# A transformer block on one core: the last batch's softmax denominators through TensorE, and new order lists

## Chip, core, metric

The kernel runs on one core of a Trainium2 chip. The metric is the device time of one execution in microseconds; lower is better. "Batch" is one of 32 sequences of 512 tokens with 256 features.

## The reference

```python
x = x + layernorm(attention(layernorm(x)))         # x: (32, 512, 256) float32
x = x + layernorm(ffn(layernorm(x)))

# attention, 16 heads of 16 features, weights 256x256 but W_down 256x64, W_up_k and W_up_v 64x256
q = x @ Wq
latent = (x @ Wk + x @ Wv) @ W_down_kv
k, v = latent @ W_up_k, latent @ W_up_v
scores = clip(q k^T / 16) * exp(-0.01 * 0.01 * |i - j|)      # 512 x 512 for each head
out = (softmax(scores) v) @ Wo

# ffn: Hadamard rotation, activations rounded to 4 bits per token, ternary weights
xh = x @ H
scale = max|xh| over the token / 7
out = (clip(round(xh / scale), -8, 7) * scale) @ ternary(weight).T
```

## The kernel before

Each engine walks its own list and meets the others at semaphores. A batch's attention is 32 **steps** (h = 0 to 31), four to a pair of heads: `scores` (L707) writes one unit of score blocks to PSUM; the unit of every fourth step holds the diagonal blocks, which VectorE multiplies by the decay (`weigh_diagonal`, L1253) and ScalarE turns into exponentials for two pairs together (`diag_exp`, L916); of the other units ScalarE takes the exponential straight from PSUM (`off_exp`, L909). Two halves of `scores_ps` alternate, so step h waits until the unit of step h - 2 has been read. `pv` (L720) multiplies four heads' exponentials (a quad) with v, in four pieces, one for each tile of 128 keys; the value matrix has an extra column of ones for each head, so row 16 of each head's 32 rows is the sum of its exponentials. VectorE copies a quad to `heads` (L1150).

Between the steps stand the other stages, of several batches at once: "pre" for the next batch (transposes `xT` L587, `lat` L595, `q` L603, `k` L614, `v` L625, with VectorE's weighting L1161, its cast L1168 and the split into two float16 parts on GpSimd L1038), "own" (scores, `pv`), "a" for the batch before (the last quad's `pv_end` and copy, the division by the sums, `y` L635 with Wo, layer norm, residual), "b" for the one before that (`x1T` L650, `x1_low` L1204, Hadamard `xh` L660, `act_scales`, rounding on ScalarE, `qintT` L669), and "c" (ternary product `z` L678, layer norm, residual, store). The tables TENSOR_STEPS, SCALAR_STEPS and VECTOR_STEPS say behind which step each engine does which piece; POOL_STEPS and SYNC_STEPS are plain sequences for one batch. Twenty-six batches run in a hardware loop of two, six are written out. Behind the last batch's scores the CLOSING lists take over: each entry is (stage, batches back from 32, half, part, piece), and the last batch (back = 1) goes in halves of two token tiles. Three PSUM banks serve the side stages in the loop, seven in the closing; `claim` waits until a bank's former holder has been taken. These banks follow from the order of the list; for the stages of the loop they are the same before and after.

**The division.** Softmax is divided by its sums after the product with v. The sums lie on one partition per head with 512 tokens along it. SyncE writes them to memory (`gather_den`, L462), loads them packed over 128 partitions (`pack_den`, L467), VectorE inverts them (`den_invert`, L1172), SyncE writes them back (`return_den`, L481) and loads them spread over the 16 rows of each head (`spread_den`, L489), and GpSimd multiplies (`heads_normalize`, L1043) the compacted heads (`compact`, L474). Then `heads_ready` lets `y` start. This is done for every batch, the last included.

## Time and profile before

| | |
|---|---|
| median of 3 runs | 1435.21 us (1431.94 to 1436.89) |
| the profiled execution | 1435.05 us, its span 1433.2 us |
| TensorE matmul busy | 1349.5 us, 94% of the span |
| TensorE weight load busy | 600.5 us, 42% |
| VectorE busy | 1179.9 us, 82% |
| ScalarE busy | 1098.2 us, 77% |
| GpSimd busy | 834.7 us, 58% |

The profile is of one execution. Times in its rows are microseconds from the start of the span. PE is TensorE's matmul, PEld its weight load, DVE VectorE, ACT ScalarE, POOL GpSimd, SPq SyncE's DMA queue, L a line of the kernel. A row of a timeline merges neighbouring instructions of one line: its length is from the first start to the last end, and matmuls of neighbouring rows overlap by their drain, so what a group costs the queue is read from its start to the next row's start. A float32 matmul appears as two instructions. PEclk is the granted clock of TensorE as a share of full speed. A square bracket is the idle time ahead of the row and what ended it.

### The profile page before, as it was taken

Reading aid. Unit: us, or ns where it says so; the run is one execution under the profiler, and the core shown is the slowest. Engines: PE = TensorE matmul, PEld = TensorE weight load, DVE = VectorE, ACT = ScalarE, POOL = GpSimd, SP = SyncE. Lnnn points to the kernel's source line nnn. Section 1 sums busy time; section 2 is a strip of 40 time slices with the busy share of each in tenths; the row PEclk is TensorE's granted clock in tenths of the full one; section 3 lists DMA queues with packets and bytes.
Section 4 is the critical chain, followed back from the end, with each engine's and each line's share of the span. In section 5 each row is a group of like instructions: output and inputs, shape, how many; then the busy total and the mean of one; then the engine's idle time right before and its main releaser. Section 6 shows DMA issues by size and latency. Waiting matters only on the chain.

```text
span 1433.2 us, 35971 instructions
## 1 busy us (share of the span) xinstructions
PE 1349.5 (94%) x12330; PEld 600.5 (42%) x12330; DVE 1179.9 (82%) x2739; ACT 1098.2 (77%) x1125; POOL 834.7 (58%) x1238
## 2 busy tenths in 40 slices
PE   5889999999999999999999999999999999999863
PEld 3334444444444444444444444444444444443332
DVE  7567888888888888888888888888888888888655
ACT  1878787888888788878878887887888787787831
POOL 4223655666565666556557655656765655675446
PEclk9999999999999999999999999999999999999986
DMA  6455456556555645656564565655556555555420
GB/s 194 154 167 170 154 172 202 155 164 206 164 182 173 197 156 166 206 157 190 173 190 157 173 201 157 193 175 187 156 177 194 163 185 184 176 156 175 128 77 31
DMA packets 174557, 241.45 MB, mean 168 GB/s; under 512 B 28336, under 2 KB 145200, under 8 KB 174512
## 3 DMA queue, kind: packets, MB, share of 16 engines
q1 hardware_dynamic: 140176, 206.78, 46.5%
q10 hardware_dynamic: 34336, 34.08, 7.7%
q8 instruction: 27, 0.44, 0.1%
q14 instruction: 18, 0.15, 0.0%
HBM read 154.80 MB, written 69.21 MB: 156 GB/s over the span
## 4 chain that ended last, share of the span: by engine, by line
PE 76%; DVE 8%; issue 5%; ACT 4%; DMA 3%; SPq 2%; POOL 2%; DVEq 0%; ACTq 0%; POOLq 0%
PE heads_ps L720 27%; PE scores_ps L707 16%; PE misc_ps L603 8%; PE misc_ps L635 7%; PE misc_ps L660 4%; PE misc_ps L614 3%; PE misc_ps L587 3%; ACT probs L909 2%; DVE x_hl L1204 2%; PE misc_ps L595 2%; PE misc_ps L678 2%; DVE diagonal L1253 2%; DVE weighted L1161 2%; PE misc_ps L625 2%; PE misc_ps L669 1%
## 5 line engine op out<-in xcount | busy, mean ns | idle before, releaser
L909 ACT ACTIVATE probs<-scores_ps 128x1024 f32<-128x1024 f32 x768 | 759.8, 1026 | 248.0 <-PE scores_ps L707 247.9
L720 PE MATMUL heads_ps<-probs,v_sb 128*32 128x512 f32 x4096 | 525.4, 603 | 3.6 <-DVE heads L1150 1.9
L1253 DVE TENSOR_TENSOR diagonal<-scores_ps,comp 128x1024 f32<-128x1024 f32 x256 | 312.2, 1219 | 70.1 <-PE scores_ps L707 70.1
L707 PE MATMUL scores_ps<-q_rep,k_rep 64*128 64x128 f16 (+2 forms) x5120 | 324.6, 251 | 16.0 <-DVE diagonal L1253 9.2
L707 PEld LDWEIGHTS scores_ps<-q_rep,k_rep 64*128 64x128 f16 x5120 | 165.6, 94 | 348.7 <-DVE diagonal L1253 149.5
L916 ACT ACTIVATE probs<-diagonal 128x2048 f32<-128x2048 f32 x128 | 246.0, 1922 | 0.0
L996 POOL TENSOR_TENSOR ln_neg_mean<-zero,ln_moments 128x4 f32<-128x4 f32 (+1 forms) x131 | 34.6, 264 | 356.5 <-DVE ln_moments L1115 356.3
L1161 DVE SCALAR_TENSOR_TENSOR weighted<-misc_ps,edges 128x384 f32<-128x384 f32 x256 | 129.4, 547 | 64.3 <-PE misc_ps L603 33.8
L720 PEld LDWEIGHTS heads_ps<-probs,v_sb 128*32 128x32 f32 x4096 | 91.5, 108 | 171.7 <-issue 169.8
L1038 POOL TENSOR_TENSOR q_hl<-weighted,q_hl 128x768 f16<-128x768 f32 x64 | 105.5, 1648 | 77.5 <-DVE q_hl L1168 77.5
L1043 POOL TENSOR_TENSOR heads_c<-heads_c,den_spread 128x1024 f32<-128x1024 f32 (+1 forms) x33 | 75.7, 2296 | 111.0 <-DMA den_spread<-den_scratch 111.0
L635 PE MATMUL misc_ps<-wo,heads_c 128*128 128x256 f32 x504 | 126.2, 393 | 1.7 <-POOL heads_c L1043 1.7
L603 PE MATMUL misc_ps<-xT,wq 128*128 128x512 f32 x256 | 126.8, 618 | 0.9 <-DVE xT L1127 0.9
L1038 POOL TENSOR_TENSOR k_hl<-weighted,k_hl 128x768 f16<-128x768 f32 x64 | 107.1, 1674 | 12.5 <-DVE k_hl L1168 12.5
L1150 DVE COPY heads<-heads_ps 128x512 f32<-128x512 f32 x128 | 87.2, 681 | 29.8 <-PE heads_ps L720 29.8
L1003 POOL TENSOR_TENSOR ln_rstd<-ln_var_eps,minus_half 128x4 f32<-128x4 f32 (+1 forms) x98 | 98.3, 1003 | 7.7
L635 PEld LDWEIGHTS misc_ps<-wo,heads_c 128*128 128x128 f32 x504 | 91.3, 191 | 25.0 <-issue 12.7
L1021 POOL TENSOR_SCALAR xn<-x_in,ln_neg_mean,ln_rstd 128x256 f32<-128x256 f32 x128 | 85.1, 677 | 0.0
L1056 POOL TENSOR_TENSOR out_sb<-out_sb,x 128x1024 f32<-128x1024 f32 (+1 forms) x33 | 81.3, 2465 | 2.8
L1052 POOL TENSOR_SCALAR out_sb<-ffn,ln_rstd,ln_shift 128x256 f32<-128x256 f32 x128 | 80.0, 640 | 0.0
L888 ACT ACTIVATE ffn<-misc_ps,magic,xscale_inv 128x256 f32<-128x256 f32 x122 | 62.3, 571 | 14.1 <-DVE xscale_inv L1220 14.1
L1029 POOL TENSOR_SCALAR y_sb<-x,ln_neg_mean,ln_rstd 128x256 f32<-128x256 f32 x128 | 69.6, 561 | 0.0
(132 smaller groups left out, 1511.5 us busy)
## 6 DMA issues: line engine op xcount, KB each, us to landing
q_rep<-q_scratch SPq DMA_DIRECT2D x128, 384.0 KB, 4.3
k_rep<-k_scratch SPq DMA_DIRECT2D x256, 192.0 KB, 3.9
q_scratch<-q_hl SPq DMA_DIRECT2D x64, 384.0 KB, 2.6
k_scratch<-k_hl SPq DMA_DIRECT2D x64, 384.0 KB, 3.1
x_in<-in_L_attn_x_dram ACTq DMA_DIRECT2D x32, 512.0 KB, 4.9
heads_c<-heads SPq DMA_DIRECT2D x256, 64.0 KB, 2.5
x_res<-in_L_attn_x_dram ACTq DMA_DIRECT2D x32, 512.0 KB, 6.8
den_spread<-den_scratch SPq DMA_DIRECT2D x256, 64.0 KB, 2.3
```

Of the source, the lines that this page charges most:

```text
L603: ins = mm(misc_ps[:, BANK["q", part], :], wq[:, piece, part * P:(part + 1) * P], xT[:, piece, :], start=(piece == 0), stop=(piece == DC - 1))
L635: ins = mm(tokens(bank_of("y", part, b))[:, piece, :], heads_c[:, c, t * P:(t + 1) * P], wo[:, c, :], start=(c == 0), stop=(c == DC - 1))
L707: ins = mm(scores_ps[:, place + par, at:at + n * P], k_rep[rows, pair, kv_, k_cols], q_rep[rows, pair, qv_, q_cols], start=True, stop=True)
L720: ins = mm(heads_ps[W32 * g:W32 * (g + 1), :], v_sb[:, b.slot, kt, at:at + W32], probs[:, quad % 2, g, kt, :], start=(kt == 0), stop=(kt = ...
L909: nc.scalar.activation(flat[:, :, at:at + S], scores_ps[:, place:place + 2, :], ACT.Exp, scale=EXP_SCALE).then_inc(off_probs, 1)
L916: nc.scalar.activation(dst, src, ACT.Exp, scale=EXP_SCALE).then_inc(diag_probs, 1)
L1003: nc.gpsimd.tensor_tensor(root, m["var_eps"][:, rows], minus_half[:, rows], ALU.pow).then_inc(ln_rstd[n], 1)
L1021: ins = nc.gpsimd.tensor_scalar(xn[:, t, :], x_in[:, t, :], m["neg_mean"][:, t:t + 1], m["rstd"][:, t:t + 1], ALU.add, ALU.mult)
L1038: nc.gpsimd.tensor_tensor(hl[:, c, 1], src, hl[:, c, 0], ALU.subtract).then_inc(split_done, 1)
L1150: v.tensor_copy(heads[:, hq, :], heads_ps[:]).then_inc(heads_taken, 1)
L1161: ins = v.scalar_tensor_tensor(weighted[:, at % 2, ver * EDGE:(ver + 1) * EDGE], bank[:, ver * P:ver * P + EDGE], gain, edges[:, ver, :], ...
L1253: v.tensor_tensor(diagonal[:, quad % 2, 2 * two:2 * two + 2, :], scores_ps[:, place:place + 2, :], comp[:].rearrange("p t n -> p (t n)").u ...
```

## The change

For the last batch alone the sums no longer go through memory. TensorE multiplies `heads` (as the stationary operand, 128 token columns at a time) by the four columns of the identity that select the four rows of sums: that turns them, token by partition, into a PSUM bank (`den`). VectorE inverts them and copies each 16 times side by side (`den_take`, into the buffer that `den_spread` was), TensorE transposes that back (`turned`), and VectorE multiplies the compacted heads by it straight from PSUM (`normalize`), in two halves. In the loop the path through memory stays. All lists, those of the loop too, are laid out anew.

```diff
 TENSOR_STEPS = {
-    1: [("z", 0, 0), ("z", 1, 0), ("pv_end", 3, 0)], 3: [("xT", 0, 0), ("pv_end", 3, 1)], 5: [("xT", 1, 0), ("pv_end", 3, 2)],
-    7: [("pv_end", 3, 3), ("lat", 0, 0)], 9: [("q", 0, 0), ("q", 0, 1)], 11: [("pv", 0, 0), ("x1T", 0, 0)],
-    13: [("x1T", 1, 0), ("pv", 0, 1)], 15: [("k", 0, 0), ("pv", 0, 2), ("k", 1, 0), ("pv", 0, 3)], 17: [("v", 0, 0), ("xh", 0, 0)],
-    19: [("xh", 1, 0), ("pv", 1, 0)], 21: [("pv", 1, 1), ("pv", 1, 2)], 23: [("q", 1, 0), ("q", 1, 1), ("pv", 1, 3)],
-    25: [("y", 0, 0), ("y", 0, 1)], 27: [("pv", 2, 0), ("qintT", 0, 0)], 29: [("y", 1, 0), ("y", 1, 1)],
+    1: [("z", 0, 0), ("z", 1, 0), ("pv_end", 3, 0)], 3: [("xT", 0, 0), ("pv_end", 3, 1)], 5: [("pv_end", 3, 2), ("xT", 1, 0)],
+    7: [("pv_end", 3, 3), ("lat", 0, 0)], 9: [("q", 0, 0), ("q", 0, 1)], 11: [("pv", 0, 0)], 12: [("x1T", 0, 0), ("x1T", 1, 0)],
+    14: [("pv", 0, 1), ("k", 0, 0)], 15: [("pv", 0, 2), ("k", 1, 0)], 17: [("pv", 0, 3), ("v", 0, 0), ("xh", 0, 0)],
+    19: [("xh", 1, 0), ("pv", 1, 0)], 21: [("pv", 1, 1), ("pv", 1, 2), ("pv", 1, 3)], 23: [("q", 1, 0), ("y", 0, 0)],
+    25: [("q", 1, 1), ("y", 0, 1)], 27: [("pv", 2, 0), ("qintT", 0, 0)], 29: [("y", 1, 0), ("y", 1, 1)],
     31: [("pv", 2, 1), ("pv", 2, 2), ("pv", 2, 3)],
 SCALAR_STEPS = {
-    4: [("load_res", 0)], 12: [("x1T", 0)], 14: [("x1T", 1)], 15: [("load_x", 0)], 21: [("round_x", 0)],
-    22: [("round_x", 1), ("round_x", 2), ("round_x", 3)], 30: [("qintT", 0)],
+    4: [("load_res", 0)], 12: [("x1T", 0), ("x1T", 1)], 13: [("load_x", 0)],
+    22: [("round_x", 0), ("round_x", 1), ("round_x", 2), ("round_x", 3)], 28: [("qintT", 0)],
 VECTOR_STEPS = {
-    1: [("z", 0), ("z", 1), ("x1_make",)], 2: [("xT", 0)], 5: [("x1_stats",), ("xT", 1), ("x1_moments",), ("z_stats",)],
-    8: [("heads_end", 3)], 10: [("lat", 0), ("q_split", 0), ("z_moments",)],
-    15: [("x1_low", 0), ("x1_low", 1), ("k_split", 0), ("den_invert",), ("k_split", 1)], 17: [("v", 0)],
-    18: [("heads", 0), ("act_scales",)], 20: [("v", 1), ("x_stats",), ("x_moments",), ("q_split", 1)], 25: [("heads", 1)],
-    26: [("quantize",)], 27: [("y", 0)], 28: [("y", 1), ("y_stats",), ("y_moments",), ("heads", 2)],
+    0: [("z", 0)], 1: [("x1_make",), ("xT", 0)], 2: [("z", 1)], 4: [("x1_stats",), ("xT", 1), ("x1_moments",), ("z_stats",)],
+    6: [("lat", 0)], 9: [("heads_end", 3)], 10: [("q_split", 0)],
+    14: [("x1_low", 0), ("x1_low", 1), ("z_moments",), ("k_split", 0), ("den_invert",), ("k_split", 1)],
+    17: [("v", 0), ("heads", 0), ("x_stats",)], 18: [("act_scales",)], 22: [("v", 1)],
+    25: [("heads", 1), ("quantize",), ("x_moments",), ("q_split", 1)], 27: [("y", 0)],
+    30: [("y", 1), ("y_stats",), ("y_moments",), ("heads", 2)],
-POOL_STEPS = ["x1_apply", ("q", 0), "rstd4", "add_out", ("k", 0), "heads_normalize", ("k", 1), "x_apply", ("q", 1), "rstd2"]
+POOL_STEPS = ["x1_apply", ("q", 0), "rstd4", "add_out", ("k", 0), "heads_normalize", ("k", 1), "x_apply", "rstd2", ("q", 1)]
-SYNC_STEPS = [("own", "spread", 1), ("a", "gather_den"), ("a", "pack_den"), ("pre", "store_q", 0), ("a", "compact", 1),
-              ("a", "return_den"), ("a", "spread_den"), ("pre", "store_k", 0), ("pre", "spread", 0), ("own", "compact", 0),
-              ("pre", "store_q", 1), ("pre", "store_k", 1), ("c", "store_out")]
+SYNC_STEPS = [("own", "spread", 1), ("a", "gather_den"), ("a", "pack_den"), ("a", "compact", 1), ("a", "return_den"),
+              ("a", "spread_den"), ("c", "store_out"), ("pre", "store_q", 0), ("pre", "store_k", 0), ("pre", "spread", 0),
+              ("own", "compact", 0), ("pre", "store_k", 1), ("pre", "store_q", 1)]
 TENSOR_CLOSING = [
+    ("pv_end", 1, None, 3, 0), ("pv_end", 1, None, 3, 1), ("pv_end", 1, None, 3, 2), ("pv_end", 1, None, 3, 3), ("den", 1, None, 0, 0),
+    ("den", 1, None, 1, 0), ("z", 3, None, 0, 0), ("z", 3, None, 1, 0), ("turned", 1, None, 0, 0), ("turned", 1, None, 1, 0),
+    ("x1T", 2, None, 0, 0), ("x1T", 2, None, 1, 0), ("y", 1, 0, 0, 0), ("y", 1, 0, 0, 1), ("y", 1, 1, 1, 0), ("xh", 2, None, 0, 0),
+    ("y", 1, 1, 1, 1), ("xh", 2, None, 1, 0), ("qintT", 2, None, 0, 0), ("z", 2, None, 0, 0), ("z", 2, None, 1, 0), ("x1T", 1, 0, 0, 0),
...
 VECTOR_CLOSING = [
+    ("x1_make", 2, None), ("x1_stats", 2, None), ("x1_moments", 2, None), ("heads_end", 1, None, 3), ("den", 1, None, 0),
+    ("den", 1, None, 1), ("z", 3, None, 0), ("normalize", 1, 0), ("z", 3, None, 1), ("normalize", 1, 1), ("x1_low", 2, None, 0),
+    ("z_stats", 3, None), ("z_moments", 3, None), ("x1_low", 2, None, 1), ("act_scales", 2, None), ("y", 1, None, 0), ("y_stats", 1, 0),
...
 POOL_CLOSING = [
-    ("x1_apply", 2, None), ("rstd4", 3, None), ("add_out", 3, None), ("heads_normalize", 1, 0), ("heads_normalize", 1, 1),
-    ("rstd2", 1, 0), ("rstd2", 1, 1), ("x1_apply", 1, 0), ("x1_apply", 1, 1), ("rstd4", 2, None), ("add_out", 2, None), ("rstd4", 1, 0),
+    ("x1_apply", 2, None), ("rstd4", 3, None), ("add_out", 3, None), ("rstd2", 1, 0), ("rstd2", 1, 1), ("x1_apply", 1, 0),
...
 SYNC_CLOSING = [
-    ("gather_den", 1, None), ("pack_den", 1, None), ("return_den", 1, None), ("compact", 1, None, 1), ("spread_den", 1, None),
-    ("store_out", 3, None), ("store_out", 2, None), ("store_out", 1, 0), ("store_out", 1, 1),
+    ("compact", 1, None, 1), ("store_out", 3, None), ("store_out", 2, None), ("store_out", 1, 0), ("store_out", 1, 1),
...
+            def den_stage(b, part, piece):
+                pe.wait_ge(heads_taken, count(HQ, b, 3 + part))
+                bank = claim("den", part, b)
+                for hq in (range(3), range(3, HQ))[part]:
+                    for t in range(T):
+                        at = 4 * (T * hq + t)
+                        ins = mm(whole(bank)[:, at:at + 4], heads[:, hq, t * P:(t + 1) * P], ident[:, HD:P:W32], start=True, stop=True)
+                ins.then_inc(in_psum["den"], 1)
+
+            def turned_stage(b, part, piece):
+                pe.wait_ge(taken["den"], 2)
+                bank = claim("turned", part, b)
+                for t in range(T):
+                    ins = nc.tensor.transpose(whole(bank)[:, t * P:(t + 1) * P], inv_rows[:, part, t, :], ident[:])
+                ins.then_inc(in_psum["turned"], 1)
...
+            def den_take(b, part):
+
+                dve.wait_ge(in_psum["den"], part + 1)
...
+                v.reciprocal(den_inv[:, at:upto], whole(bank_of("den", part, b))[:, at:upto]).then_inc(den_inverse, 1)
+                dve.wait_ge(den_inverse, part + 1)
+                for hq in (range(3), range(3, HQ))[part]:
+                    half, c = divmod(hq, 2)
+                    dst = inv_rows[:, c, :, 64 * half:64 * half + 64].rearrange("p t (g d) -> p t g d", d=HD)
+                    src = den_inv[:, 4 * T * hq:4 * T * (hq + 1)].rearrange("p (t g) -> p t g", g=4).unsqueeze(3).to_broadcast([P, T, 4, HD])
+                    ins = v.tensor_copy(dst, src)
+                ins.then_inc(taken["den"], 1)
+
+            def normalize(b):
+                dve.wait_ge(heads_compacted, count(128, b, 128))
+                dve.wait_ge(in_psum["turned"], 2)
+                for c in range(DC):
+                    ins = v.tensor_tensor(heads_c[:, c, b.columns], heads_c[:, c, b.columns], whole(bank_of("turned", c, b))[:, b.columns], ALU.mult)
+                ins.then_inc(heads_ready, 1)
```

## Rows read from the trace of the kernel before

**Rows 1.** Windows: the 28 whole batches; columns: length, busy (count) per engine, PEclk, DMA.

```profile
154.40:1328.00 1173.60, 1155.93 (x10716) 511.08 (x10711) 1009.60 (x2333) 953.12 (x978) 725.25 (x1054) 1.00 0.57 177
```

**Rows 2.** Timeline of TensorE in one batch: start, length, line, operation, shapes, [idle before].

```profile
743.83 1.05 PE L678 MATMUL misc_ps<-ternary,x_hl 128*128 128x256 bf16 x8
...
746.35 0.66 PE L587 MATMUL misc_ps<-ident,xn 128*128 128x128 f32 x4
...
758.52 1.07 PE L720 MATMUL heads_ps<-probs,v_sb 128*32 128x512 f32 x8
759.52 0.61 PE L707 MATMUL scores_ps<-q_rep,k_rep 64*128 64x256 f16 x8
760.38 0.70 PE L614 MATMUL misc_ps<-latT,w_up_k 64*128 64x256 f32 x4 [0.25 <-DVE x_hl L1204]
...
762.24 0.70 PE L614 MATMUL misc_ps<-latT,w_up_k 64*128 64x256 f32 x4 [0.16 <-DVE weighted L1161]
...
769.38 1.92 PE L720 MATMUL heads_ps<-probs,v_sb 128*32 128x512 f32 x16
771.24 0.61 PE L707 MATMUL scores_ps<-q_rep,k_rep 64*128 64x256 f16 x8
771.78 1.98 PE L603 MATMUL misc_ps<-xT,wq 128*128 128x512 f32 x4
...
775.24 1.99 PE L635 MATMUL misc_ps<-wo,heads_c 128*128 128x256 f32 x8
777.17 0.61 PE L707 MATMUL scores_ps<-q_rep,k_rep 64*128 64x256 f16 x8
777.84 1.06 PE L720 MATMUL heads_ps<-probs,v_sb 128*32 128x512 f32 x8
```

**Rows 3.** Waits of TensorE over the 28 batches: total, times, longest.

```profile
PE misc_ps L614 <- DVE x_hl L1204: 7.1, 28, 0.3
PE misc_ps L614 <- DVE weighted L1161: 4.6, 28, 0.2
```

**Rows 4.** Timeline of VectorE, same batch.

```profile
758.89 1.39 DVE L1204 TENSOR_TENSOR x_hl<-misc_ps,x_hl 128x512 f16<-128x512 f32 x2
...
762.65 0.55 DVE L1172 RECIPROCAL den_inv<-den_packed 128x64 f32<-128x64 f32 x1
...
777.02 0.67 DVE L1150 COPY heads<-heads_ps 128x512 f32<-128x512 f32 x1
```

**Rows 5.** Timeline of SyncE's queue, same batch.

```profile
763.22 0.33 SPq L481 DMA_DIRECT2D den_scratch<-den_inv  x1
766.04 3.59 SPq L489 DMA_DIRECT2D den_spread<-den_scratch  x8
```

**Rows 6.** Timeline of GpSimd, same batch.

```profile
771.56 2.37 POOL L1043 TENSOR_TENSOR heads_c<-heads_c,den_spread 128x1024 f32<-128x1024 f32 x1 [3.05 <-DMA den_spread<-den_scratch]
```

**Rows 7.** Chain that ended last, after the last product with the values: start, length, what.

```profile
1376.30 0.70 DVE heads L1150
...
1394.39 3.05 PE scores_ps L635 x8
```

**Rows 8.** Timeline of the end, all engines.

```profile
1406.30 0.20 POOL L996 TENSOR_TENSOR ln_neg_mean<-zero,ln_moments 128x2 f32<-128x2 f32 x1
...
1413.80 2.34 POOL L1056 TENSOR_TENSOR out_sb<-out_sb,x 128x1024 f32<-128x1024 f32 x1
...
1413.82 2.35 DVE L1217 TENSOR_SCALAR xscale<-absmax 128x2 f32<-128x2 f32 x1
```

**Rows 9.** Windows at the end, columns as in rows 1.

```profile
1376.00:1380.00 4.00, 0.78 (x8) 0.31 (x4) 3.70 (x9) 0.00 (x0) 0.00 (x0) 1.00 0.02 6
```

**Rows 10.** Another window at the end.

```profile
1377.00:1406.30 29.30, 12.45 (x56) 9.20 (x56) 18.24 (x61) 4.15 (x7) 17.80 (x37) 0.75 0.26 67
```

**Rows 11.** Timeline of the weight setup at the start, TensorE.

```profile
7.75 1.08 PE L759 MATMUL scores_ps<-ident,x 128*128 128x128 f32 x4 [7.75 <-DVE x L1323]
...
9.97 1.97 PE L766 MATMUL scores_ps<-w_down,out_sb 128*128 128x64 f32 x8 [1.13 <-DVE out_sb L1327]
```

More of the change, by code:

```diff
@@ L55, in count @@
     return per_batch * batch.number + done
-PARTS = {"xT": 2, "x1T": 2, "lat": 1, "xh": 2, "q": 2, "k": 2, "qintT": 1, "y": 2, "z": 2, "v": 2}
+PARTS = {"xT": 2, "x1T": 2, "lat": 1, "xh": 2, "q": 2, "k": 2, "qintT": 1, "y": 2, "z": 2, "v": 2, "den": 2, "turned": 2}
 DISTANCE_OF = {"load": 2, "pre": 1, "own": 0, "a": -1, "b": -2, "c": -3}
@@ L65 @@
     **dict.fromkeys(("heads", "pv"), "own"),
-    **dict.fromkeys(("pv_end", "heads_end", "load_res", "den_invert", "heads_normalize", "y", "y_stats", "y_moments", "rstd2"), "a"),
+    **dict.fromkeys(("pv_end", "heads_end", "load_res", "den_invert", "heads_normalize", "y", "y_stats", "y_moments", "rstd2", "den", "turned", "normalize"), "a"),
     **dict.fromkeys(("x1_make", "x1_stats", "x1_moments", "rstd3", "x1_apply", "x1T", "x1_low", "xh", "act_scales",
@@ L112 @@
 VECTOR_CLOSING = [
-    ("z", 3, None, 0), ("heads_end", 1, None, 3), ("x1_make", 2, None), ("z", 3, None, 1), ("x1_stats", 2, None),
-    ("x1_moments", 2, None), ("z_stats", 3, None), ("den_invert", 1, None), ("z_moments", 3, None), ("x1_low", 2, None, 0),
-    ("x1_low", 2, None, 1), ("act_scales", 2, None), ("quantize", 2, None), ("y", 1, None, 0), ("y_stats", 1, 0), ("y_moments", 1, 0),
-    ("y", 1, None, 1), ("y_stats", 1, 1), ("x1_make", 1, 0), ("y_moments", 1, 1), ("z", 2, None, 0), ("x1_stats", 1, 0),
@@ L117 @@
-    ("x1_moments", 1, 0), ("z", 2, None, 1), ("x1_make", 1, 1), ("x1_stats", 1, 1), ("x1_moments", 1, 1), ("z_stats", 2, None),
-    ("z_moments", 2, None), ("x1_low", 1, 0, 0), ("x1_low", 1, 1, 1), ("act_scales", 1, 0), ("act_scales", 1, 1), ("quantize", 1, 0),
-    ("quantize", 1, 1), ("z", 1, None, 0), ("z_stats", 1, 0), ("z_moments", 1, 0), ("z", 1, None, 1), ("z_stats", 1, 1),
-    ("z_moments", 1, 1),
+    ("x1_make", 2, None), ("x1_stats", 2, None), ("x1_moments", 2, None), ("heads_end", 1, None, 3), ("den", 1, None, 0),
@@ L121 @@
+    ("den", 1, None, 1), ("z", 3, None, 0), ("normalize", 1, 0), ("z", 3, None, 1), ("normalize", 1, 1), ("x1_low", 2, None, 0),
+    ("z_stats", 3, None), ("z_moments", 3, None), ("x1_low", 2, None, 1), ("act_scales", 2, None), ("y", 1, None, 0), ("y_stats", 1, 0),
[3 rows of a table added]
+    ("act_scales", 1, 1), ("quantize", 1, 0), ("quantize", 1, 1), ("z", 1, None, 0), ("z_stats", 1, 0), ("z_moments", 1, 0),
+    ("z", 1, None, 1), ("z_stats", 1, 1), ("z_moments", 1, 1),
 ]
 POOL_CLOSING = [
-    ("x1_apply", 2, None), ("rstd4", 3, None), ("add_out", 3, None), ("heads_normalize", 1, 0), ("heads_normalize", 1, 1),
@@ L377, in part_count @@
         def part_count(stage, b, part):
+            if stage in ("den", "turned"):
+                return part + 1
             return PARTS[stage] * (b.made if GROUP[stage] == "pre" else b.number) + part + 1
@@ L724, in _ @@
             stages = {"xT": xT_stage, "lat": lat_stage, "q": q_stage, "k": k_stage, "v": v_stage, "y": y_stage,
-                      "x1T": x1T_stage, "xh": xh_stage, "qintT": qintT_stage, "z": z_stage, "pv": pv, "pv_end": pv}
+                      "x1T": x1T_stage, "xh": xh_stage, "qintT": qintT_stage, "z": z_stage, "pv": pv, "pv_end": pv,
+                      "den": den_stage, "turned": turned_stage}
             def iteration(loop, offset, present):
@@ L1238, in z_moments @@
                 ln_moments_of(4, b)
-            steps = {"x_stats": x_stats, "x_moments": x_moments, "xT": xT_take, "lat": lat_take, "v": v_take, "y": y_take,
+            steps = {"den": den_take, "normalize": normalize, "x_stats": x_stats, "x_moments": x_moments, "xT": xT_take, "lat": lat_take, "v": v_take, "y": y_take,
                      "q_split": lambda b, part: weigh(b, "q", part), "k_split": lambda b, part: weigh(b, "k", part),
```

17 lines of the change are left out of this document (14 added, 3 removed), and 9 rows, old and new, of tables (TENSOR_CLOSING, VECTOR_CLOSING).

## The prediction

> **What bounds the kernel now.** I read the windows of the 28 whole batches first. They take 1173.60 us, 41.91 us a batch. TensorE is busy for 1155.93 us of it (98.5%), VectorE for 86%, ScalarE for 81%, at the full granted clock [rows 1]. So in the loop TensorE's queue is the bound, and only two things in the lists can shorten a batch: time in which TensorE stands, and the short cost of each switch from one kind of matmul to another. The waits of TensorE say how much it stands: the two products of `k_stage` wait 7.1 and 4.6 us in 28 batches, 0.42 us a batch [rows 3]. Its timeline shows a little more, from start to start. A pair of score units takes 0.54 us where nothing waits (771.24 to 771.78), but 0.86 us before the first k product and 0.67 us before the product at 777.84 [rows 2], which waits for the copy of `heads` of 777.02 to 777.69 [rows 4]. That is 0.32 and 0.13 us lost, and 0.2 us at the second k product, 0.65 us together.
>
> The end is another regime. The chain of waits goes from the last copy of `heads` (1376.30) through memory to the multiplication on GpSimd and to `y_stage` at 1394.39 [rows 7]: 18.1 us. The fixed tail behind it begins with GpSimd's layer norm work on the second half's `x1_moments` at 1406.30 [rows 8] and runs to the end of the span, 1433.2 - 1406.3 = 26.9 us. I take that tail as it is, since its operations and their order are kept.
>
> **The loop, part by part.** The same instructions are issued; only places change.
> - Both `x1T` come together at step 12 and `k` at 14 and 15. VectorE now has step 12's diagonal, then both `x1_low` (1.39 us) [rows 4], and the k products find their banks emptied: the two waits go, -0.5 us. The next thing late is step 14, whose scores need step 12's diagonal, with only the two x1T groups, some 1.1 us, between: +0.1.
> - `pv` 1,3 joins 1,1 and 1,2. Two pieces apart take 1.00 us each (758.52 to 759.52), two together 1.86 us (769.38 to 771.24) [rows 2], so a switch costs 0.14 us: -0.14. The two x1T in one run save another switch, -0.14; the score units of 12 and 15 each now stand alone or in new pairs, one run more, +0.2.
> - `pv` 2,0 finds its bank emptied, because the copy of `heads` 1 comes a diagonal earlier than it is needed: -0.13.
> - `q` 1 and `y` 0 are cut into halves and paired, q with y. Both are 128x128 float32 products, and I take no switch between them. The trace before has no such neighbours: the bounds are 0 and one switch of up to 0.2 us at two places (the 0.14 us above, with a margin). The upper end would be +0.4; I take 0, as the nearest case, the two halves of z with their own waits (8 instructions, 1.05 us, one run) [rows 2], shows no break.
> - `lat` on VectorE moves ahead of step 8's diagonal, a copy of some 0.4 us, and `z` 1 stands between x1_make and the copies of xT: VectorE has no idle time from step 0 to 12, and `lat_stage` waits for the second xT copy some 0.1 us.
> - The first piece of y now comes 2.0 us earlier. It needs the multiplied heads. Before, return_den was issued at 763.22, spread_den at 766.04, and the multiplication ended at 771.56 + 2.37 = 773.93 [rows 5, 6]; y started at 775.24 [rows 2], so 1.3 us were spare. In the new lists `den_invert` (762.65 before) [rows 4] comes about 0.6 us earlier, since its k product and k_split come earlier, and no `store_q` stands ahead of the compacting DMAs. Against that the last copy of `heads` stands behind `lat`, some 0.4 us later, but the inversion waits for the k product, not for it. Spare: 1.3 + 0.6 - 2.0 = -0.1, with the scatter of DMAs a wait of 0.2 us.
> - SyncE: `store_out` moves from the end to ahead of `store_q`, `store_k` and `spread`. The 512 KB of out are queued behind the spread of the denominators, not before, and the q and k copies for the next batch still land about 4 us before the next step 0. ScalarE's load of x comes two steps earlier, where its buffer is long free. GpSimd's rstd2 goes ahead of the last split, whose store is needed only at step 16 of the next batch. I cost these at 0; the cover is that slack of 4 us and more, and if it were gone each us would be paid in every batch.
>
> Sum: -0.5 - 0.13 - 0.14 - 0.14 + 0.2 + 0.1 + 0.1 + 0.2 = -0.3; following the whole batch with these durations, queue by queue, I come out between -0.3 and -0.5, and take -0.4 us a batch, 28 x 0.4 = -11 us. With all bounds at their bad end a batch is +0.2 (both switches at 0.2, waits twice as long), with all at the good end -0.75.
>
> In the batches at both edges, where some groups are missing, TensorE runs ahead, and the earlier y waits longer for the heads: about +2 us over three of them.
>
> **The end.** Removed: four gathering DMAs, pack, reciprocal of 0.55 us, return, eight spreading DMAs, two multiplications on GpSimd. Added, in order:
> - 16 float32 products with 4 columns each. Float32 products are two instructions in this trace, so 24 for the first part and 8 for the second. No row has such narrow ones. Nearest above: eight instructions with 64 columns in 1.90 us (1.97 with the drain) [rows 11], 0.24 each; nearest below in shape: four float32 transposes in 0.66 us [rows 2], 0.14 each from start to start. With 0.24 it is 7.6 us, with 0.11 (the weights alone of these transposes) 3.4. The setup ran slower: four transposes took 1.08 us there [rows 11] and take 0.66 in the loop, although its record shows no lower clock. At 1376 to 1380 the granted clock is still full [rows 9], with TensorE idle, so I halve the setup's 0.24 and take 0.12: 2.9 us and 1.0 us, and the sums stand at 1379.4 and 1380.3.
> - VectorE: two reciprocals (0.55 us for 64 columns as a bound for both, plus 0.2), four copies of 128x256, 0.4 us each by the 0.67 us of a 128x512 copy [rows 4], 2.3 us in all, done at 1381.6.
> - Eight transposes, two groups of 0.6 us as the same kind takes in the loop [rows 2]: the first is done at 1382.8, both at 1383.
> - VectorE multiplies, two pieces of 0.4 us for each half: the first half stands at 1383.7 to 1384, against just before 1394.39. Compacting is four DMAs issued from 1377.0 (2.4 us) and landing 2.5 us later, 1382, and is hidden by this.
>
> So y can start 10.4 us earlier. How much of it arrives? From 1377.0 to 1406.3 VectorE was busy for 18.24 us of 29.3 [rows 10]. Now x1_make, x1_stats and x1_moments of the batch before the last go ahead of the last heads copy (into a gap) and den_invert goes, -3.9; the copies, reciprocals (+2.3) and multiplications (+1.7) come, and z_stats and z_moments of the batch before the last now stand ahead of the last x1_moments (+1.8): 20.1 us. The waits that stay: 2.4 for the sums, 0.7 for the transposes, 2.4 for xh of the batch before the last (act_scales stands ahead of the first y copy in VectorE's list, and xh behind three quarters of y on TensorE), 0.8 behind add_out on GpSimd, 0.5 of small ones, 6.8 us. The second x1_moments then ends at 1377.0 + 26.9 = 1403.9, not 1406.2: the end gains 2.3 us, because VectorE's list becomes the bound where memory was. With 7.6 us of products it gains 0 and at worst loses 2.
>
> The Trainium skill, "TensorE: Matmul & The Clock Gate", section "LDWEIGHTS (loading the stationary operand)", has a weight load go by its columns over 1.2, 107 ns for 128, whatever the width of the product. With two loads per product an estimate by that page is 32 x 0.107 = 3.4 us for the sums, half a microsecond below mine.
>
> Sum: the profiled execution took 1435.05 us (span 1433.2), the median of the runs is 1435.21. 1435.05 - 11 + 2 - 2.3 = 1423.8, say 1424.
>
> **Rivals.**
> - *The loop gains nothing.* The halves of q and y cost a switch each, and the waits return elsewhere in VectorE's packed first half. For it: TensorE is already at 98.5%. Against: the k waits are in all 28 batches [rows 3]. Then 1435 + 2 - 2.3, about 1434.5.
> - *The earlier y waits for the heads, through memory, in every batch.* Price: if the multiplication ends at the same place in the batch as before, y waits 2.0 - 1.3 = 0.7 us, and if the later last copy of `heads` carries through, 1.1 us, against the 0.6 us otherwise gained. Above 0.6 us of waiting the change is slower. 28 x 0.3 = 8 us, less the tail and plus the edges: about 1442. For it: the chain of DMAs has the least slack in the batch, and the start of the multiplication already scatters by some tenths. Against: the inversion comes earlier.
> - *The end gains in full.* If VectorE's other work fits into waits, all 10 us arrive: 1416. Against: the 18.24 us of rows 10.
> - *GpSimd holds up VectorE in the end.* In the trace a 128x2 operation of VectorE lasted 2.35 us, just as long as GpSimd's addition of 2.34 us that began with it [rows 8]. The same addition for batch 29 now falls at about 1392.6 to 1395, next to act_scales, and the new copies lie from SBUF to SBUF. If it hits, the 2.3 us are gone: 1426. The Trainium skill, "SBUF — State Buffer", section "Terms", calls the two engines' shared ports exclusive, held for a whole instruction; by that rule the row is no accident, and the trace agrees.
>
> **How the numbers follow.** Forecast 46%, own range 1417 to 1430; loop gains nothing 20%; y waits 17%; full gain 10%; GpSimd holds up 7%. I call a difference below 0.3% (4.3 us, 1431 to 1439.5) no change. Forecast, full gain and GpSimd give faster, and a part of the second case, 0.67; same 0.16, slower 0.17. The range goes from 1413 to 1441.
>
> **What would show it.** Right: the windows give 41.3 to 41.6 us a batch; the waits of L614 vanish from TensorE's list; the first multiplied half stands near 1384 less the loop's gain, while layer norm of the second half starts only 2 us earlier relative to the last `pv_end`. Wrong: waits of the y products for GpSimd's heads_c over 0.6 us a batch, or a batch of 41.9 with the k waits gone, which would be switches; in the end, 0.2 us per narrow product and a lower granted clock from 1377 on.

## The result

The changed kernel is slower: 1479.3 us in the median of four runs (1469.5 to 1483.7) against 1435.1 us before, a ratio of 1.030 (1.024 to 1.036). The forecast was 1424 us, its range ended at 1441. The profiled execution took 1469.47 us, its span 1467.7 us.

The end did what was forecast; the loop did not. From the end of the last product with the values to the end of the span it is 1467.7 - 1413.0 = 54.7 us after and 1433.2 - 1376.2 = 57.0 us before: 2.3 us gained. In the 24 middle batches, measured from one start of `z` to the next, a batch takes 43.53 us after and 41.93 before ([rows 1] has 41.91 for 28).

### The profile page after: what moved, and what is told of

It reads as the page before. It is cut to its first block, busy times and chain, and to the rows that moved or that the text cites. A ratio compares the mean times of both kernels' runs of the same rounds, so it can differ in the third digit from the quotient of the medians.

```text
span 1467.7 us, 36050 instructions
## 1 busy us (share of the span) xinstructions
PE 1363.1 (93%) x12370; PEld 617.2 (42%) x12370; DVE 1217.2 (83%) x2748; ACT 1101.3 (75%) x1125; POOL 812.2 (55%) x1236
## 4 chain that ended last, share of the span: by engine, by line
PE 52%; DVE 25%; DMA 8%; issue 8%; SPq 4%; POOL 2%; ACT 2%; DVEq 0%; POOLq 0%
PE heads_ps L744 16%; PE scores_ps L731 11%; PE misc_ps L659 8%; DVE diagonal L1303 7%; PE misc_ps L627 6%; DVE ln_stats L1132 6%; DMA den_packed<-den_scratch 3%; DMA den_scratch<-heads 2%; SPq L467 2%; DVE weighted L1186 2%; DVE v_sb L1163 2%; PE misc_ps L702 2%; DVE absmax L1261 2%; DVE heads L1175 2%; PE misc_ps L611 1%
## 5 line engine op out<-in xcount | busy, mean ns | idle before, releaser
L744 PE MATMUL heads_ps<-probs,v_sb 128*32 128x512 f32 x4096 | 518.4, 601 | 3.2 <-ACT probs L941 1.6
L731 PE MATMUL scores_ps<-q_rep,k_rep 64*128 64x128 f16 (+2 forms) x5120 | 335.7, 252 | 47.3 <-DVE diagonal L1303 41.0
L1021 POOL TENSOR_TENSOR ln_neg_mean<-zero,ln_moments 128x4 f32<-128x4 f32 (+1 forms) x131 | 26.7, 204 | 503.3 <-DVE ln_moments L1140 503.2
L1186 DVE SCALAR_TENSOR_TENSOR weighted<-misc_ps,edges 128x384 f32<-128x384 f32 x256 | 128.1, 542 | 28.7 <-PE misc_ps L638 21.5
L627 PE MATMUL misc_ps<-xT,wq 128*128 128x512 f32 x256 | 141.5, 657 | 1.9 <-DVE xT L1152 0.9
L659 PE MATMUL misc_ps<-wo,heads_c 128*128 128x256 f32 x512 | 136.9, 402 | 4.3 <-POOL heads_c L1068 4.3
L659 PEld LDWEIGHTS misc_ps<-wo,heads_c 128*128 128x128 f32 x512 | 98.2, 198 | 53.7 <-issue 35.4
L1175 DVE COPY heads<-heads_ps 128x512 f32<-128x512 f32 x128 | 87.4, 683 | 27.8 <-PE heads_ps L744 26.3
L1068 POOL TENSOR_TENSOR heads_c<-heads_c,den_spread 128x1024 f32<-128x1024 f32 x31 | 73.4, 2368 | 23.1 <-DMA den_spread<-den_scratch 22.7
L1081 POOL TENSOR_TENSOR out_sb<-out_sb,x 128x1024 f32<-128x1024 f32 (+1 forms) x33 | 76.0, 2302 | 2.8
L1046 POOL TENSOR_SCALAR xn<-x_in,ln_neg_mean,ln_rstd 128x256 f32<-128x256 f32 x128 | 69.9, 559 | 0.0
L1168 DVE COPY y_sb<-misc_ps 128x512 f32<-128x512 f32 x64 | 44.0, 687 | 27.0 <-PE misc_ps L659 27.0
```

The lines of the kernel that those rows point to most:

```text
L627: ins = mm(misc_ps[:, BANK["q", part], :], wq[:, piece, part * P:(part + 1) * P], xT[:, piece, :], start=(piece == 0), stop=(piece == DC - 1))
L659: ins = mm(tokens(bank_of("y", part, b))[:, piece, :], heads_c[:, c, t * P:(t + 1) * P], wo[:, c, :], start=(c == 0), stop=(c == DC - 1))
L731: ins = mm(scores_ps[:, place + par, at:at + n * P], k_rep[rows, pair, kv_, k_cols], q_rep[rows, pair, qv_, q_cols], start=True, stop=True)
L744: ins = mm(heads_ps[W32 * g:W32 * (g + 1), :], v_sb[:, b.slot, kt, at:at + W32], probs[:, quad % 2, g, kt, :], start=(kt == 0), stop=(kt = ...
L1175: v.tensor_copy(heads[:, hq, :], heads_ps[:]).then_inc(heads_taken, 1)
L1186: ins = v.scalar_tensor_tensor(weighted[:, at % 2, ver * EDGE:(ver + 1) * EDGE], bank[:, ver * P:ver * P + EDGE], gain, edges[:, ver, :], ...
```

## Profile after: the loop

The window of the 24 middle batches of the changed kernel (columns as in [rows 1]):

```profile
283.83:1328.61 1044.78, 1004.13 (x9221) 451.14 (x9217) 905.43 (x2017) 823.40 (x841) 609.00 (x913) 0.99 0.53 171
```

TensorE now stands for 41 us of 1045, and its clock is 0.99. From start to start of `z` the batches fall on three levels: four of 24 at 41.46 to 41.66 us, twelve at 43.2 to 43.4, eight at 44.8 to 45.0. The waits of TensorE, 160 to 1340 us (total, times, longest):

```profile
PE scores_ps L731 <- DVE diagonal L1303: 35.7, 20, 1.9
PE misc_ps L649 <- DVE weighted L1186: 2.1, 7, 0.7
PE misc_ps L659 <- POOL heads_c L1068: 1.1, 1, 1.1
PE misc_ps L619 <- DVE xT L1152: 0.4, 2, 0.2
```

The k waits of [rows 3] are gone. In their place stands one wait of 1.8 us in 20 batches: the scores of step 22 for VectorE's diagonal of step 20. VectorE's timeline of such a batch says why that diagonal is late:

```profile
779.82 1.21 DVE L1303 TENSOR_TENSOR diagonal<-scores_ps,comp 128x1024 f32<-128x1024 f32 x1
780.95 0.74 DVE L1163 COPY v_sb<-misc_ps 128x256 f32<-128x256 f32 x2
781.61 0.68 DVE L1175 COPY heads<-heads_ps 128x512 f32<-128x512 f32 x1
782.21 1.39 DVE L1132 BATCH_NORM_STATS2 ln_stats<-x_in 128x6 f32<-128x256 f32 x4
783.52 1.27 DVE L1261 TENSOR_REDUCE absmax<-misc_ps 128x2 f32<-128x512 f32 x2
784.82 0.66 DVE L1267 TENSOR_SCALAR xscale<-absmax 128x4 f32<-128x4 f32 x1
785.51 0.18 DVE L1270 RECIPROCAL xscale_inv<-xscale 128x4 f32<-128x4 f32 x1
785.61 2.28 DVE L1271 TENSOR_TENSOR xscale_sq<-xscale 128x4 f32<-128x4 f32 x1
787.81 1.21 DVE L1303 TENSOR_TENSOR diagonal<-scores_ps,comp 128x1024 f32<-128x1024 f32 x1
```

The square of 4 elements in a row (`xscale_sq`, last line of `act_scales`) lasts 2.28 us; over 28 batches of the kernel before it is 0.13 us on average. Now GpSimd, same stretch:

```profile
781.47 2.37 POOL L1081 TENSOR_TENSOR out_sb<-out_sb,x 128x1024 f32<-128x1024 f32 x1
783.80 1.65 POOL L1063 TENSOR_TENSOR k_hl<-weighted,k_hl 128x768 f16<-128x768 f32 x1
785.51 2.36 POOL L1068 TENSOR_TENSOR heads_c<-heads_c,den_spread 128x1024 f32<-128x1024 f32 x1
787.83 1.64 POOL L1063 TENSOR_TENSOR k_hl<-weighted,k_hl 128x768 f16<-128x768 f32 x1
```

Lay the two side by side. `xscale` begins inside the k split and ends at 785.48, within 0.03 us of its end (785.45). The square begins 0.10 us after the multiplication of the heads and ends at 787.89, as that does (787.87). The reciprocal between them is not held. Before, the multiplication waited for its DMA in all 28 batches, 87.3 us in total, and began 1.9 to 4.4 us after the square in all but the last; after, it waits in five batches (160 to 1340 us), 4.8 us.

The third level is the clock. Windows of TensorE's wait and the 2 us behind it, first in a batch of 43.25 us, then in one of 44.9:

```profile
787.20:789.00 1.80, 0.02 (x3) 0.00 (x0) 1.80 (x3) 0.46 (x2) 1.80 (x2) 1.00 0.70 282
789.00:791.00 2.00, 1.87 (x12) 1.07 (x13) 0.69 (x3) 1.49 (x2) 0.47 (x1) 1.00 0.67 220
830.50:832.30 1.80, 0.03 (x4) 0.00 (x0) 1.80 (x3) 0.51 (x2) 1.80 (x2) 1.00 0.73 288
832.30:834.30 2.00, 1.91 (x10) 0.94 (x11) 0.64 (x2) 1.53 (x2) 0.42 (x1) 0.76 0.67 208
834.30:836.30 2.00, 2.00 (x5) 1.00 (x3) 0.00 (x0) 2.00 (x2) 0.00 (x0) 0.50 0.99 314
```

Both waits are alike; behind the second the granted clock falls to 0.50, the lower of the two levels (1.2 GHz), and the next q half takes 1.76 us instead of 1.13. It fell behind 8 of the 20 waits, and these are the eight batches of 44.9. The sum closes: 35.7 + 8 x 1.6 = 48.5 us, 2.0 us a batch over 24, and 43.53 - 2.0 = 41.5 is the forecast batch. The profiled execution is the shortest of the four; the others are 6 to 14 us longer at a mean granted clock of 0.970 to 0.975 against its 0.976. More batches of the third level would fit that, but those executions have no trace.

## Profile after: the end

The chain that ended last (start, length, what) at the last product with the values, then VectorE's timeline; they answer to [rows 7, 8].

```profile
1409.36 3.64 PE heads_ps L744 x32
1413.00 3.67 PE misc_ps L589 x32
```

```profile
1417.03 0.25 DVE L1204 RECIPROCAL den_inv<-misc_ps 128x16 f32<-128x16 f32 x1
1417.31 0.29 DVE L1210 COPY den_spread<-den_inv 128x256 f32<-128x256 f32 x1
1417.52 0.68 DVE L1280 TENSOR_TENSOR ffn<-misc_ps,wscale_rows 128x512 f32<-128x512 f32 x1
1419.76 0.75 DVE L1217 TENSOR_TENSOR heads_c<-heads_c,scores_ps 128x256 f32<-128x256 f32 x2 [1.56 <-PE scores_ps L596]
```

The 32 narrow products take 3.7 us, and the first multiplied half stands at 1420.5, 7.5 us after the last product with the values; before, it was 18.1 us until `y` could start. The layer norm of the second half starts 27.8 us after it, against 30.1.

## Experiments

Every run has its own runs of the kernel before on the same chip. "A batch" is the mean of the 24 middle ones in the profiled execution, "the end" the time from the last product with the values to the end of the span.

**The end alone, the square alone, the multiplication in halves, SyncE alone.**

```diff
e1   TENSOR/SCALAR/VECTOR/POOL/SYNC_STEPS of the kernel before, the rest as changed
e2   def act_scales:  - v.tensor_tensor(xscale_sq[...], xscale[...], xscale[...], ALU.mult)
     def quantize:    + v.tensor_tensor(xscale_sq[...], xscale[...], xscale[...], ALU.mult)
e3   def heads_normalize:  - tensor_tensor(heads_c[:, :, ...])   + for c in range(DC): tensor_tensor(heads_c[:, c, ...])
e4   SYNC_STEPS of the kernel before
```

> The five lists of the loop are those of the kernel before; the closing lists and the new functions are the changed kernel's. Theory (the end gained 2.3 us as forecast and the loss lies wholly in the loop's lists): 1435.1 - 2.3 = 1432.8 us, 41.9 us a batch, the square of the scales 0.13 us in all batches. Rival (the new end, or the banks that the closing order gives the loop, costs time): 1440 us or more.

Measured 1434.9 us against 1437.0, ratio 0.999 (0.9975 to 1.000); a batch 41.94 us, the square 0.13 us. The medians differ by 2.1 us, at the edge of the interval; in the trace the end takes 56.0 us against 57.0, with the narrow products at a granted clock of 0.81 (4.5 us instead of 3.7). So the end is worth 1 to 2 us, and the whole loss is the loop's.

> The changed kernel with one 128x4 operation of VectorE (xscale_sq) moved from the end of act_scales (step 18) to behind quantize (step 25), where GpSimd is idle. Theory (VectorE stands there until GpSimd's heads_c multiplication ends, 2.2 us for an operation of 0.13 us; TensorE then waits 1.8 us, and its clock falls after that wait): all batches come to 41.5 us, no batch of 43.3 or 44.9, granted clock 1.00, some 1421 us (1417 to 1427). Rival 1 (the order of the new lists itself costs the time, VectorE's list being too full between steps 14 and 20): at most 0.13 us a batch, 1465 to 1480. Rival 2 (the clock falls by itself, not because of the wait): batches of 41.5 and of 43.1.

Measured 1422.5 us, ratio 0.990 (0.987 to 0.992); a batch 41.52 us, none of 43 or more; the waits for the diagonal are down to one of 1.1 us:

```profile
285.57:1282.01 996.44, 989.27 (x9221) 444.27 (x9217) 861.62 (x2017) 821.96 (x841) 611.59 (x913) 1.00 0.56 179
```

Moving one operation of 0.13 us gives back 57 us of medians (the ratio goes from 1.030 to 0.990; the changed kernel itself ran on another chip), and lands on the forecast. Both rivals fall, the second because the clock stays at 1.00.

> The changed kernel with GpSimd's heads_c multiplication (one of 128x1024, 2.36 us) as two of 128x512. Theory (VectorE is held for one whole instruction of GpSimd, and is let in at its end): the square lasts 1.0 to 1.2 us instead of 2.2, TensorE waits 0.7 us instead of 1.86 in these batches, and the clock does not fall after so short a wait: batches of 41.5 and 42.2, 1433 to 1442 us. Rival (VectorE is held until GpSimd's queue has a gap, or by the data itself): square 2.2 us as before or longer, 1470 to 1480.

Measured 1434.9 us, ratio 0.998 (0.996 to 0.999). VectorE and GpSimd in one of its batches:

```profile
732.38 0.18 DVE L1272 RECIPROCAL xscale_inv<-xscale 128x4 f32<-128x4 f32 x1
732.47 1.10 DVE L1273 TENSOR_TENSOR xscale_sq<-xscale 128x4 f32<-128x4 f32 x1
```

```profile
730.67 1.65 POOL L1063 TENSOR_TENSOR k_hl<-weighted,k_hl 128x768 f16<-128x768 f32 x1
732.28 2.50 POOL L1069 TENSOR_TENSOR heads_c<-heads_c,den_spread 128x512 f32<-128x512 f32 x2
```

The square gets in between the two halves. TensorE waits 0.62 to 0.87 us in 17 batches, the granted clock is 1.00 behind every one that the trace shows, and the levels are 41.6 and 42.2 us. Half the instruction costs a quarter of the price (42.06 - 41.52 = 0.54 us a batch instead of 2.0), because the clock no longer falls, 17 batches are held and not 20, and TensorE has 0.4 us to spare at that place: a square 2.1 us late lengthened a batch by 1.7 us, one 1.0 us late by 0.6.

> The changed kernel with SyncE's list of the kernel before (store_q ahead of the compacting DMAs, store_out at the end). Theory (two edits together bring square and multiplication together: x_stats ahead of act_scales makes the square 1.4 us later, SyncE's list makes the multiplication 1.3 us earlier): the multiplication starts 1.3 us later again, 7.0 us after the start of step 16's diagonal, the square is 0.13 us in most batches, y waits 0.2 to 0.3 us: 41.6 to 41.9 a batch, 1426 to 1437 us. Rival (the multiplication starts when GpSimd has ended its first k_split, whatever SyncE does): no change, 1470 to 1480.

Measured 1420.5 us, ratio 0.988 (0.986 to 0.990), somewhat better than expected: a batch 41.36 us. The multiplication waits for its DMA in 28 batches again (22.3 us) and mostly starts 0.2 to 0.9 us after the square, which is free in all but the last. VectorE and GpSimd in one batch:

```profile
767.16 0.13 DVE L1271 TENSOR_TENSOR xscale_sq<-xscale 128x4 f32<-128x4 f32 x1
```

```profile
767.95 2.38 POOL L1068 TENSOR_TENSOR heads_c<-heads_c,den_spread 128x1024 f32<-128x1024 f32 x1 [0.95 <-DMA den_spread<-den_scratch]
```

So SyncE's list is one of the edits that bring them together, and the margin is a few tenths of a microsecond. It does not move the multiplication by the 1.3 us that I expected: on average over the 24 batches that starts 6.3 us after step 16's diagonal, against 5.6 in the changed kernel and 6.9 before. SyncE's list makes 0.7 us of the 1.3; the rest comes with the other lists (the inversion stands 0.3 us earlier).

**The scales earlier, the collision put into the kernel before, both cures, the halves unpaired.**

```diff
e5  VECTOR_STEPS  - 17: [("v", 0), ("heads", 0), ("x_stats",)], 18: [("act_scales",)], 22: [("v", 1)]
                  + 17: [("v", 0), ("heads", 0)], 18: [("act_scales",)], 22: [("v", 1), ("x_stats",)]
e6  kernel before, VECTOR_STEPS  - 20: [("v", 1), ("x_stats",), ("x_moments",), ...]
                                 + 20: [("v", 1), ("x_stats",), ("square",), ("x_moments",), ...]   (and no square in step 18)
e7  e2 and e4 together
e8  e7, TENSOR_STEPS  - 23: [("q", 1, 0), ("y", 0, 0)], 25: [("q", 1, 1), ("y", 0, 1)]
                      + 23: [("q", 1, 0), ("q", 1, 1)], 25: [("y", 0, 0), ("y", 0, 1)]
```

> The changed kernel with x_stats back behind act_scales (step 22, behind v 1), so that the scales of the activations come 1.4 us earlier on VectorE, as in the kernel before. Theory (VectorE waits for GpSimd's instructions, whose places do not change): the earlier xscale now meets the first k_split (3.98 to 5.63 us after the start of step 16's diagonal), is held to its end, and the square meets the multiplication as in the changed kernel: 2.1 to 2.3 us in most batches, 1465 to 1485 us, no gain. Rival (x_stats ahead of act_scales is what makes the diagonal late): 1.4 us a batch back, 1425 to 1435 us.

Measured 1441.7 us (1426 to 1449), ratio 1.001 (0.9985 to 1.004): between the two. VectorE and GpSimd in a batch that was held:

```profile
562.91 1.67 DVE L1267 TENSOR_SCALAR xscale<-absmax 128x4 f32<-128x4 f32 x1
564.62 0.18 DVE L1270 RECIPROCAL xscale_inv<-xscale 128x4 f32<-128x4 f32 x1
564.72 2.30 DVE L1271 TENSOR_TENSOR xscale_sq<-xscale 128x4 f32<-128x4 f32 x1
```

```profile
562.91 1.65 POOL L1063 TENSOR_TENSOR k_hl<-weighted,k_hl 128x768 f16<-128x768 f32 x1
564.63 2.36 POOL L1068 TENSOR_TENSOR heads_c<-heads_c,den_spread 128x1024 f32<-128x1024 f32 x1
```

The mechanism is as I said: an earlier scale is only held longer by the k split (1.2 us on average), and then meets the multiplication all the same. The count was not: the square is held for 2.2 us or more in eight batches and by the k split for 1.4 in six. In the others the multiplication came after the square, mostly by a few tenths, since it waited for its DMA. The order of two starts within 0.1 us decides about 2 to 3.5 us.

> The kernel before with the square of the scales moved from the end of act_scales to behind x_stats (step 20), 3.5 us later, where GpSimd's multiplication runs, but where VectorE has 1.0 us to spare ahead of q_split. Theory: the square lasts 1.3 to 1.5 us instead of 0.13 in the batches in which the multiplication has begun, q_split comes 0.3 to 0.5 us late, and nearly nothing arrives at TensorE: 1435 to 1440 us. Rival 1 (a held VectorE costs its whole wait wherever it falls): 28 x 1.3 = 36 us more, 1471. Rival 2 (no holding: the square was long in the changed kernel for a reason of its own): 0.13 us, 1435.

Measured 1435.8 us against 1436.1, ratio 0.999 (0.998 to 1.001). The square is long in 27 of 28 batches, 1.38 us on average, and lasts to the end of the multiplication (773.67 + 2.36 = 776.03):

```profile
773.34 1.40 DVE L1107 BATCH_NORM_STATS2 ln_stats<-x_in 128x6 f32<-128x256 f32 x4
774.65 1.41 DVE L1224 TENSOR_TENSOR xscale_sq<-xscale 128x4 f32<-128x4 f32 x1
```

```profile
773.67 2.36 POOL L1043 TENSOR_TENSOR heads_c<-heads_c,den_spread 128x1024 f32<-128x1024 f32 x1 [2.87 <-DMA den_spread<-den_scratch]
```

35 us of held VectorE cost nothing, since q_split had a microsecond to spare. The hold is a fact of the two instructions; its price is the place. The statistics ahead of it, which start before the multiplication and run beside it, take their usual 1.4 us.

> Both cures: the changed kernel with SyncE's list of the kernel before and the square behind quantize. With SyncE's list alone the multiplication started only 0.2 to 0.9 us after the square, so the square was already free. Theory: 41.25 to 41.4 us a batch, 1419 to 1421 us, no difference from SyncE's list alone that can be measured. Rival (SyncE's list helps by something else, and the two gains add up): 1410 or less.

Measured 1421.0 us, ratio 0.9895 (0.988 to 0.991): as expected, the cures do not add up.

> Both cures, and the halves of q 1 and y 0 not paired but one whole after the other (q, q at step 23, y, y at step 25). The prediction took a change between q and y at no cost, with a bound of 0.4 us a batch. Theory (no switch among them; starts are 0.96 us apart in either order): within 0.1 us a batch of both cures, 1417 to 1423 us. Rival (a switch from q to y costs 0.14 us twice): 28 x 0.28 = 8 us less, 1412.

Measured 1412.9 us, ratio 0.983 (0.981 to 0.985); a batch 41.29 us, nearly all of them 41.25. The number is the rival's, the reason is not: e7 too has batches of 41.25 us, and from the q half to the y half it is 0.96 us there, no switch. Beside them e7 has batches in which y starts up to 0.4 us late for `heads_c`, 0.10 us on average. Unpaired, the first y stands two steps later and never waits. A batch is 0.15 us shorter, the stretch from the first `z` to the 29th 5.2 us. The opening ahead of it differs by another 1.5, but it scatters by 4 us between the profiled executions of e8 to e12, which share it (153.8 to 158.1). The remaining 1.4 us of the 8.1 between the medians have no explanation in the traces.

**The end.** In e8 the 128x2 `xscale` of the last half took 2.03 us beside GpSimd's addition of `out` for batch 30.

```diff
e9   def add_out (for batch 30)  + pool.wait_ge(xscale_ready, closing(1, 1).done)   ahead of the addition
e10  e9, VECTOR_CLOSING: z_stats, z_moments of batch 29 ahead of the multiplied heads; y's first half ahead of act_scales
     of batch 30; the second half's layer norms ahead of z of batch 30
e11  e10, the wait is for qint_ready (the last quantize)
e12  e8 again
```

> The kernel with both cures and unpaired halves (its end took 54.5 us from the last product with the values), and in the closing the addition of out for the batch before the last waits until VectorE has made the last scales. There the 128x2 xscale took 2.03 us (1392.47), begun 0.33 us after that addition of GpSimd (2.34 us, at 1392.14). Theory (VectorE is held by GpSimd in the end too, and the chain from xscale to the last store pays it in full; the addition has 4.8 us of room behind): xscale 0.2 us, the end 1.8 to 1.9 us shorter, 52.6 us, some 1411 us. Rival (a 128x2 operation in this place lasts 2 us for another reason, its own wait or its place in VectorE's queue): no change, 54.5 us, 1413.

Measured 1413.4 us, ratio 0.983 (0.982 to 0.985): no gain over e8's ratio of 0.983, although the scale took 0.17 us. VectorE behind it, and GpSimd:

```profile
1391.85 0.17 DVE L1270 TENSOR_SCALAR xscale<-absmax 128x2 f32<-128x2 f32 x1
1392.06 0.17 DVE L1273 RECIPROCAL xscale_inv<-xscale 128x2 f32<-128x2 f32 x1
1392.57 2.22 DVE L1277 TENSOR_SCALAR x_hl<-ffn 128x512 bf16<-128x512 f32 x1 [0.35 <-ACT ffn L913]
```

```profile
1392.17 2.34 POOL L1083 TENSOR_TENSOR out_sb<-out_sb,x 128x1024 f32<-128x1024 f32 x1 [0.74 <-DVE xscale L1270]
```

The hold moved to the next operation that can be held, the quantize, which is on the same chain. My expectation looked at one victim.

> The same with VectorE's closing list in another order: z_stats and z_moments of batch 29 ahead of the multiplications of the heads, y's first half taken ahead of act_scales of batch 30, and the second half's layer norms ahead of z of batch 30. Theory (after the change VectorE's list is the bound between the multiplied heads and the layer norm, so that most of the 10.4 us gained by the earlier heads is lost in it; GpSimd's out of batch 29, which x1_make waits for, comes 3.5 us earlier): the end 3 to 4 us shorter again, 49 to 50 us, some 1408 us. Rival (the order in VectorE's list is hidden behind TensorE's xh and the exponent function of ScalarE): no change beside the run with the later addition alone.

Measured 1412.3 us, ratio 0.982 (0.980 to 0.983), 1.1 us below e9, inside the scatter of both. The end is 53.5 us against 56.5 in e9; in both the clock was 0.75 to 0.76 during the narrow products (4.8 us instead of 3.7). The quantize was held again, 2.09 us.

> The last kernel again, but GpSimd's addition of out for batch 30 now waits for the last quantize instead of the last scales. In the two runs before, the scale took 0.17 us, but the next operation of VectorE of that kind, the first half's quantize (0.41 us), took 2.09 and 2.22 us beside the addition: the hold had only moved. Theory: the first quantize takes 0.41 us, the last scale 0.17 us; the addition fits ahead of the last z_moments; from the last layer norm work on the first half of x1 (L1055) to the end 1.6 us shorter; the end 52 us or a little less, 1409 to 1411 us. Rival (another bound stands behind, the exponent power and scalings on GpSimd or ScalarE's rounding): no gain, 1412.3 us.

Measured 1408.4 us (1405 to 1413), ratio 0.980 (0.978 to 0.982), a little better than expected. No operation waits for that addition any more:

```profile
1389.69 0.43 DVE L1278 TENSOR_SCALAR x_hl<-ffn 128x512 bf16<-128x512 f32 x1 [0.92 <-ACT ffn L914]
```

```profile
1386.38 2.16 POOL L1078 TENSOR_SCALAR out_sb<-ffn,ln_rstd,ln_shift 128x256 f32<-128x256 f32 x4
1391.18 2.35 POOL L1084 TENSOR_TENSOR out_sb<-out_sb,x 128x1024 f32<-128x1024 f32 x1 [2.63 <-DVE x_hl L1278]
```

> The kernel of e8 once more, in five rounds beside the last one, to tell the value of the end's edits from the scatter between chips: 1412 to 1414 us, ratio 0.982 to 0.984. If the end's edits are worth what their traces show (2 to 3 us), e11 comes out below it by that.

Measured 1414.1 us, ratio 0.984 (0.982 to 0.986), as expected. The end is 54.9 us there and 50.7 us in e11; the medians on the same chip differ by 5.7, more than the 2 to 3 that I expected and than the 4.2 that the traces show. So e11 is the best version: 28.7 us below the kernel before, and some 71 below the changed one.

## Why the prediction was wrong

**What bounds the loop: right.** TensorE's queue does, and a batch without the hold comes to 41.46 to 41.66 us in the changed kernel and 41.52 on average in e2; forecast 41.5.

**The terms of the loop that were worked out: right in sum.** The k waits vanished. Between q and y there is no switch, here in the changed kernel:

```profile
789.74 1.13 PE L627 MATMUL misc_ps<-xT,wq 128*128 128x512 f32 x2
790.70 1.03 PE L659 MATMUL misc_ps<-wo,heads_c 128*128 128x256 f32 x4
791.66 0.61 PE L731 MATMUL scores_ps<-q_rep,k_rep 64*128 64x128 f16 x12
```

The earlier y was to wait 0.2 us for its heads. In e2, with the changed kernel's lists, it does not wait at all (0.96 us from q to y in all 24 batches); with SyncE's list of before, in e7, it waits 0.10 us. What I did not separate are the switches of -0.14 and +0.2 and the small waits; their sum fits.

**The step that failed** is "SyncE ... I cost these at 0", together with the silence on `x_stats` ahead of `act_scales`. I asked of each moved step only whether its data still came in time. The cover that I named was enough: TensorE has no wait for `q_rep` or `k_rep`. What I did not ask is what VectorE does while GpSimd's moved instruction runs. [rows 6] already shows that the multiplication had 3.05 us of idle time ahead of it; I credited the earlier inversion as spare time for y, but not with letting a 2.36 us instruction slide to the place where `act_scales` now ends. Two small shifts towards each other, 1.4 us of the square (0.5 of it the k split that holds `xscale`) and 1.3 us of the multiplication (0.7 by SyncE's list), close a gap of 2.5 us. What I put at 0 measured 36 us of waiting and 13 us of lower clock.

**The rival that had the mechanism stood in the wrong place.** I took the 2.35 us of [rows 8] as GpSimd holding VectorE, priced it at 2.3 us once in the end and gave it 7%. The same rule held in the loop costs 1.8 to 3.4 us in 20 batches. In the end it occurs too, before (2.35 us) and after (2.03 us) alike. And the trace of the kernel before has it inside the loop, where I did not look. In the last of its 28 batches VectorE's cast of k, otherwise 0.56 us, lasts until GpSimd's addition has ended, and TensorE waits for the diagonal behind it:

```profile
1309.37 2.46 DVE L1168 CAST k_hl<-weighted 128x768 f16<-128x768 f32 x1
```

```profile
1309.05 2.36 POOL L1056 TENSOR_TENSOR out_sb<-out_sb,x 128x1024 f32<-128x1024 f32 x1
```

```profile
1313.02 0.61 PE L707 MATMUL scores_ps<-q_rep,k_rep 64*128 64x256 f16 x8 [1.46 <-DVE diagonal L1253]
```

The first batch has the same, and these two take 43.6 us instead of 41.8. In 22 batches the cast of q, usually 0.56 us too, takes 0.8 to 1.5 us, at a place where TensorE then waits 0.4 us at most.

The Trainium skill, "SBUF — State Buffer", section "SBUF: two separate sides", says that a VectorE operation in a mode with two ports, or with two SBUF inputs beside a GpSimd operation that reads SBUF, and the GpSimd operation exclude each other: the one that starts first has the ports for its whole instruction, and the other "fully blocks". The traces agree: the square has two such inputs and is held; the reciprocal and the statistics, with one each, and the diagonal, which takes only one of its two from SBUF, keep their 0.18, 0.41 and 1.22 us beside GpSimd's `tensor_tensor`. `xscale` and the cast have one and are held, which by that rule would be such a mode; no run shows the mode itself. e3 shows "for its whole instruction": half the instruction, half the hold. Had I run that rule over the list of every batch, the slower side would have been the likeliest case.

**My other rivals.** The loop gains nothing: no. y waits for the heads: not in e2, by 0.1 us in e7, not by 0.7 to 1.1. The end gains in full: no.

**The end: right, and in the main for the reason given.** Gain 2.3 us (forecast 2.3), first multiplied half 7.5 us after the last product (forecast 7.5). The narrow products took 3.7 us (forecast 3.9). The estimate worked out from the Trainium skill, "TensorE: Matmul & The Clock Gate", section "LDWEIGHTS (loading the stationary operand)", was 3.4 us; the trace is 0.3 above. Some of the agreement is luck. The halving of 0.24 us was not worked out: the transposes that I compared differ by 1.08 to 0.66, which would give 0.15 us each and 4.7 us. Reciprocals and copies took 1.8 us, not 2.3, and the eight transposes 1.9 us at a granted clock of 0.50, not 1.2, which about cancels. That VectorE's list takes the rest fits e9 to e12: reordered alone it shortens the end by 3.0 us (e9 to e10, both at the lower clock), reordered and with the hold removed by 4.2 (e12 to e11).

**The edges**, +2 us in the forecast, were not tested by a run of their own.
